# Attention with a routed feed-forward: the softmax is normalised on GpSimd before the transposes instead of behind the product with the values

## What is computed

```python
q = (layernorm(x) @ Wq.T + bq)   # 16 heads of 32
k = (ctx @ Wk.T + bk);  v = (ctx @ Wv.T + bv)
scores = q k^T / sqrt(32) + mask
attn = softmax(scores, axis=-1)
x = x + tanh(g_xattn) * ((attn @ v) @ Wo.T + bo)
# then, on layernorm(x): gate_weights = softmax(x @ gate_w + gate_b), the two
# best of 8 experts, each a network of three layers with gelu between them
x = x + tanh(g_ffn) * sum(topk_vals * expert_out[topk_idx])
```

## Time and profile before

| | us |
|---|---|
| median of 3 runs (lowest, highest) | 1741.77 (1741.31, 1743.95) |
| the profiled execution | 1747.38 |
| its span | 1745.6 |
| TensorE busy | 1714.5 (98%) |
| VectorE busy | 1209.6 (69%) |
| ScalarE busy | 932.3 (53%) |
| GpSimd busy | 181.0 (10%) |
| granted TensorE clock, mean | 0.995 |

### The profile page before, as it was taken

The page is one execution under the profiler, slowest core; times in us unless marked ns, Lnnn a source line. Parts: engine busy times, 40 slices in busy tenths (PEclk is TensorE's granted clock), DMA queues, the critical chain, the costliest instruction groups (busy, mean ns, idle before and its releaser), DMA issues.

```text
span 1745.6 us, 40414 instructions
## 1 busy us (share of the span) xinstructions
PE 1714.5 (98%) x15462; PEld 1515.4 (87%) x15462; DVE 1209.6 (69%) x2807; ACT 932.3 (53%) x1652; POOL 181.0 (10%) x271
## 2 busy tenths in 40 slices
PE   9998999999999999999999999999999999999998
PEld 8887988898888888988897777777899999999997
DVE  5576777777777777777775555666677777777773
ACT  5654565556555655565554344545555555555551
POOL 1011110111011101110100010000000010011100
PEclk9999999999999999999999999999999999999999
DMA  7983222322132213221215299998666666766662
GB/s 247 383 313 101 72 81 60 98 73 85 56 99 74 80 59 99 72 85 55 77 34 181 74 365 395 351 349 296 218 212 204 207 210 216 223 223 221 212 199 49
DMA packets 128181, 292.72 MB, mean 168 GB/s; under 512 B 19610, under 2 KB 42842, under 8 KB 128040
## 3 DMA queue, kind: packets, MB, share of 16 engines
q1 hardware_dynamic: 104616, 225.46, 38.3%
q0 software_dynamic: 23424, 65.30, 12.6%
HBM read 244.04 MB, written 46.66 MB: 167 GB/s over the span
## 4 chain that ended last, share of the span: by engine, by line
PE 82%; DVE 8%; DMA 5%; ACT 3%; issue 2%; SPq 0%; POOLq 0%; DVEq 0%; POOL 0%; ACTq 0%
PE bank_rows L2289 21%; PE bank_rows L739 12%; PE bank_rows L725 12%; PE bank_rows L2304 7%; PE bank_rows L792 5%; PE bank_rows L2343 3%; PE bank_rows L780 3%; PE bank_rows L803 3%; PE bank_rows L2329 3%; PE bank_rows L819 3%; DVE probs L1458 3%; PE bank_rows L762 2%; PE bank_rows L2370 2%; DMA stage<-in_L_ffn_w 2%; PE bank_rows L882 2%
## 5 line engine op out<-in xcount | busy, mean ns | idle before, releaser
L1136 ACT ACTIVATE probs<-probs,neg_max 100x726 f32<-100x726 f32 x256 | 228.9, 896 | 176.2 <-DVE neg_max L1458 176.2
L1458 DVE CUSTOM_DVE_ANT_0 probs<-bank_rows,mask_sb 100x726 f32<-100x726 f32 x256 | 223.0, 909 | 23.2 <-PE bank_rows L780 20.4
L2533 DVE TENSOR_TENSOR w_low<-stage,w_high 128x1024 fp32r<-128x1024 f32 x176 | 213.4, 1223 | 36.2 <-ACT w_high L2437 35.5
L2437 ACT ACTIVATE w_high<-stage 128x1024 fp32r<-128x1024 f32 x176 | 183.6, 1057 | 33.7 <-DMA stage<-in_L_ffn_w 33.6
L2460 ACT ACTIVATE gelu<-bank_rows,biases 128x256 f32<-128x256 f32 x176 | 82.4, 475 | 216.7 <-PE bank_rows L2289 173.8
L2289 PE MATMUL bank_rows<-h_high,w_high 128*128 128x256 f32 x704 | 196.5, 279 | 0.0
L2289 PE MATMUL bank_rows<-h_low,w_high 128*128 128x256 f32 x704 | 196.5, 279 | 0.0
L2289 PE MATMUL bank_rows<-h_high,w_low 128*128 128x256 f32 x704 | 196.5, 279 | 0.0
L1142 ACT ACTIVATE p_t<-bank_rows 122x1200 f32<-122x1200 f32 x128 | 146.5, 1169 | 91.3 <-PE bank_rows L792 91.3
L725 PE MATMUL bank_rows<-ctx_high,wk_high 128*128 128x360 f32 (+1 forms) x512 | 176.9, 346 | 10.7 <-DVE v_even L1439 8.4
L725 PE MATMUL bank_rows<-ctx_low,wk_high 128*128 128x360 f32 (+1 forms) x512 | 168.9, 330 | 0.0
(11 more groups left out here) (245 smaller groups left out, 3862.3 us busy)
## 6 DMA issues: line engine op xcount, KB each, us to landing
stage<-in_L_ffn_w SPq DMA_DIRECT2D x240, 512.0 KB, 4.4
plain_w<-in_L_ffn_w SPq DMA_DIRECT2D x15, 2048.0 KB, 12.5
expert_in_rows<-filling POOLq DMA_DIRECT2D x8, 3341.0 KB, 23.0
router_rows<-in_gate_rows POOLq DMA_DIRECT2D x112, 200.0 KB, 3.6
ctx_raw<-in_ctx SPq DMA_DIRECT2D x16, 720.0 KB, 4.7
ctx_raw<-in_ctx SPq DMA_DIRECT2D x15, 724.0 KB, 4.3
xs_sb<-expert_in_rows SPq DMA_DIRECT2D x11, 514.0 KB, 5.5
b_sb<-in_L_ffn_b SPq DMA_DIRECT2D x19, 256.0 KB
```

The costliest lines, as they stand in the source:

```text
L1136: nc.scalar.activation(p, p, ACT.Exp, bias=neg_max[:, h:h + 1], scale=-1.0, accum_out=exp_sum[:, h:h + 1]).then_inc(probs_ready, 1)
L1458: nc.vector.tensor_tensor_reduce(out=pieces(probs[:, q, :]), in0=slots_of(q)[0:S, :, 0:PIECE], in1=pieces(mask_sb[:]), scale=-1.0, scalar= ...
L2437: nc.scalar.activation(hi, src, ACT.Copy).then_inc(chunk_hi[which], 1)
L2533: nc.vector.tensor_tensor(lo, src, hi.bitcast(F32), ALU.subtract).then_inc(chunk_lo[which], 1)
```

## The change

The exponentials are multiplied by the inverse of their sum before they are transposed, by GpSimd, in place. VectorE inverts the sums of a pair (`invert`, 100x2) as soon as its order comes to it, GpSimd's `divide` multiplies one head at a time, and `transpose_probs` waits for `probs_divided` instead of `probs_ready`. The transpose of the inverse, its broadcast and its copy are gone, and `scale_o` has become `copy_o`, a plain copy. In `body`, one unit stands between the two transpose runs of a group, on TensorE and in ScalarE's order. On ScalarE the key copy of the last unit is behind all four exponentials in group 1, and `route_exps` is ahead of a key copy in group 2. On GpSimd the loops over batches are written out, with the fills spread over batches 0 and 1 and the wait for them in batch 2.

```diff
@@ on_gpsimd @@
-        for e in range(E):
-            pool.wait_ge(scored, FILL_AFTER[e])
...
-        pool.wait_ge(regions_filled, 16 * E)
...
+        def divide(b, g):
+
+            for h in range(HQ * g, HQ * (g + 1)):
+                if h % 2 == 0:
+                    pool.wait_ge(sum_inverted, H // 2 * b + h // 2 + 1)
+                p = probs[:, h % HQ, :]
+                nc.gpsimd.tensor_scalar(p, p, recip[:, h:h + 1], None, ALU.mult).then_inc(probs_divided, 1)
+
+        def body(b, t):
+
+            if b == 2:
+                pool.wait_ge(regions_filled, 16 * E)
+            if b > 1:
+                scatter(t - 1)
+            if b == 1:
+                fill(E - 4)
+            divide(b, 0)
+            if b == 1:
+                fill(E - 3)
+            divide(b, 1)
+            pass_router(t, (0,))
+            pass_router(t, (1, 2))
+            if b == 1:
+                fill(E - 2)
+            divide(b, 2)
+            pass_router(t, (3,))
+            if b == 1:
+                fill(E - 1)
+            divide(b, 3)
+            pass_router(t, range(4, E if t < IN_ROWS - 1 else E - ROUTER_SLOTS))
+
+        for g in range(DT):
+            pool.wait_ge(scored, HQ * g + 1)
+            fill(g)
+            divide(0, g)
@@ on_tensor @@
         def transpose_probs(b, pair):
-            pe.wait_ge(probs_ready, H * b + 2 * pair + 2)
+            pe.wait_ge(probs_divided, H * b + 2 * pair + 2)
@@ attend @@
-            pe.wait_ge(recip_ready, DT * b + g + 1)
-            nc.tensor.transpose(bank[:, P:P + S], recip_sum[:].rearrange("s h d -> s (h d)"),
-                                ident[0:S, 0:S]).then_inc(ready, 1)
+            last.then_inc(ready, 1)
@@ body of on_tensor, group 2 @@
             transpose_probs(b, 4)
-            transpose_probs(b, 5)
             if b + 2 < B:
                 transpose_xn(b, b + 2)
             keys(b, n, *((1, 0) if odd else (0, 1)))
+            transpose_probs(b, 5)
             keys(b, n, 0 if odd else 1, 1)
@@ body of on_scalar, group 2 @@
             copy_probs(b, 4)
-            copy_probs(b, 5)
             if b + 2 < B:
                 copy_transposed(b, "XT", xt[:, :, slot(b + 2), :])
+            route_exps(t)
             keys_high(b, n, *((1, 0) if odd else (0, 1)))
-            route_exps(t)
+            copy_probs(b, 5)
             keys_high(b, n, 0 if odd else 1, 1)
@@ on_vector @@
-        def recips(b, g):
-            dve.wait_ge(probs_ready, H * b + HQ * (g + 1))
-            at = slice(HQ * g, HQ * (g + 1))
-            nc.vector.reciprocal(recip[:], exp_sum[:, at]).then_inc(recip_made, 1)
-            dve.wait_ge(recip_made, DT * b + g + 1)
-            nc.vector.tensor_copy(recip_sum[:], recip[:].rearrange("s (h a) -> s h a", a=1).broadcast_to([S, HQ, HD])
-                                  ).then_inc(recip_ready, 1)
-
-        def scale_o(body, b, g):
+        def invert(b, pair):
+
+            dve.wait_ge(probs_ready, H * b + 2 * pair + 2)
+            at = slice(2 * pair, 2 * pair + 2)
+            nc.vector.reciprocal(recip[:, at], exp_sum[:, at]).then_inc(sum_inverted, 1)
+
+        def copy_o(body, b, g):
             bank, done = take(body, f"A{g}")
-            dve.wait_ge(r_copied, DT * b + g + 1)
-            nc.vector.tensor_tensor(o_t[:, g, :], bank[:, 0:S], r_sb[:], ALU.mult).then_inc(done, 1)
+            nc.vector.tensor_copy(o_t[:, g, :], bank[:, 0:S]).then_inc(done, 1)
@@ body of on_vector, groups 2 and 3 @@
             scored_around(b, 2, b, b, 1)
+            invert(b, 4)
             keys_low(b, n, 2, 0)
+            invert(b, 5)
             dots(t, (3, 4))
-            recips(b, 2)
             values_out(b, 1 - odd, 1)
...
             scored_around(b, 3, b, b, 2)
+            invert(b, 6)
             keys_low(b, n, 3, 0)
+            invert(b, 7)
             choose(t)
-            recips(b, 3)
             values_out(b, 1 - odd, 2)
```

More of the change, by code:

```diff
@@ L936, in body @@
             transpose_probs(b, 0)
+            values(b, 4)
             transpose_probs(b, 1)
-            values(b, 4)
             values(b, 5)
@@ L949, in body @@
             transpose_probs(b, 2)
+            if odd:
+                values(b, 0)
+            else:
+                keys(b, n, 0, 0)
             transpose_probs(b, 3)
             if odd:
-                values(b, 0)
                 keys(b, n, 0, 0)
             else:
-                keys(b, n, 0, 0)
                 keys(b, n, 1, 0)
@@ L1119, in copy_transposed @@
                                  ACT.Copy).then_inc(done, 1)
-        def recip_copy(body, g):
-            bank, _ = take(body, f"A{g}")
-            nc.scalar.activation(r_sb[:], bank[:, P:P + S], ACT.Copy).then_inc(r_copied, 1)
         def queries_high(body, name):
@@ L1220, in body @@
             exps(b, 0)
-            recip_copy(b, 3)
             exps(b, 1)
@@ L1699, in first_body @@
             norm_in(1)
-            recips(b, 0)
             values_out(b, 0, 4)
@@ L1709, in first_body @@
             ctx_low(n, 3)
-            recips(b, 1)
             keys_low(b, n, 0, 0)
@@ L1802, in last_body @@
             scored_around(b, 0, b, t, 3)
+            invert(b, 0)
             keys_low(b, b, 3, 1)
-            recips(b, 0)
+            invert(b, 1)
             values_out(b, odd, 3)
```

101 lines of the change are left out of this document (49 added, 52 removed).

## The result

| | before | changed |
|---|---|---|
| median of the runs (lowest, highest), us | 1741.54 (1740.82, 1743.95) | **2085.57** (2082.75, 2091.07) |
| ratio, 95% interval | 1 | 1.1976 (1.1949 to 1.2004) |
| profiled execution and its span, us | 1747.4 and 1745.6 | 2086.4 and 2084.6 |
| busy TensorE, VectorE, ScalarE, GpSimd, us | 1714.5, 1209.6, 932.3, 181.0 | 1828.9, 1256.0, 923.7, 750.2 |
| granted TensorE clock, mean | 0.995 | 0.938 |

A forecast was written before the change was run, and what follows sets the result against it. TensorE was taken as the bound, busy 299.06 of 300 us in the attention part. Middle batches +38.5, first and last batch +21, clock +5, fills -8 gave +56.5 on 1741.8: 1798 us, range 1762 to 1832.

The forecast's parts named there:

- Part 1: Every group: the inverse is no longer transposed, giving TensorE 0 to 0.24 us a group, 0.12 taken.
- Part 2: GpSimd's 256 multiplies of 100x726: 0.85 us each, bounds 0.73 and 1.46; groups 0 to 2 lose nothing up to 0.86.
- Rival B: A slow multiply on GpSimd: at 1.1 us +29, so 1827 us; at 1.46, near 1870; chance 0.15.
- Part 3: Group 3: the choice of experts starts later and TensorE's pair count waits for it; the group ends 1.15 us later.
- Part 4: Group 2: late values and a router row reloaded behind four multiplies delay group 3's scores by 1.8 us a period.
- rival A: VectorE and GpSimd hold each other up at router dots and the choice of experts: +24.5 us, so 1823; chance 0.25.
- Part 5: First and last batch: transpose runs wait for divided pairs in eight places at 2.6 us, +21 us; clock falls, +5.
- Clock: First and last batch: TensorE's clock falls twice more after waits, +5 us, with 0 and eight falls as bounds.
- Part 6: Batch 1: a later wait for the fills, spread over two batches, shortens TensorE's gap: -8 us, bounds -4 and -9.
- the count: TensorE's count of the pairs in group 3, waiting for the choice of experts: 1.15 us later a period.
- C: Faster: freed VectorE lets inverse, multiply and router row arrive before TensorE asks; 1739 us, chance 0.06.

## Why the prediction was wrong

The sign was right, but not for the reason given: most of the cost comes from a multiply 2.6 times as long as the sum's. By its own parts:

- **Part 1** (0 to 0.24 us a group, 0.12 taken): at the low end. Without multiplies and in the old order the kernel is at 0.9981, no better than with the fills alone, 0.9988. VectorE's wait in the midst of its scores is gone, and it was off the path.
- **Part 2 is the step that failed**: "I take 0.85 us ... bounds 0.73 and 1.46". The multiply takes 2.1 us, 2.24 in the mean, outside the bounds. The memset and the copy were the nearest rows, but not an upper bound for an instruction that reads, computes and writes: its price an element is 2.51 ns, where the memset's 518 ns are 1.0 ns an element at most. An upper bound made of twice a write had no row behind it that reads a long stream on GpSimd. Rival B added 29 us to the sum for a multiply of 1.1 us, which makes 86 in all; 124 were measured at 1.17 us. That is 1866 us, near the 1870 that B gave to a multiply of 1.46.
- **The rule in part 2**, no first run of groups 0 to 2 late up to 0.86 us, held at 0.84 us: no such wait in the middle batches.
- **Part 3** (16 us): 15 us by the kernel with group 3 put back. **Part 4** (25 us): 24 us by the one with group 2 put back. But these are costs of the order, not of the multiply: they are there with no multiply at all, which the text did not see. That part 4 fits so well is in part luck, since its 25 us were worked out with a multiply of 0.85 us. With one of 0.84 us group 2 waits for 33 us, and the 8 us more are about the 9 that VectorE's dots add to the second pair (rival A).
- **Part 5** (21 us in eight places): 19.4 us in eight waits at 0.84 us. At 2.24 us batch 0 alone has 5.82, 4.08, 4.87 and 5.96 us. Clock: +5 with bounds 0 and eight falls. At the predicted length it was more: TensorE is busy for 1733.0 us at a mean clock of 0.986, and for 1716.8 at 0.995 with no multiplies, 16 us less for the same work. In the changed kernel about 8 us of every period are lower clock, which my sum had nowhere, since it had no waits of 2 to 3 us in the middle batches.
- **Part 6** (-8): -2. The text had the wait on GpSimd's side end the gap; the queue behind the fill held the row as well.

At the length that it assumed, the sum was off by 18 us. Against its terms group 2 has 8 us more, the fills 6 and the clock 11, the count 4 less and the first and last batch 2 less, which makes 19. At the real length it was off by 288, and nearly all of that is the multiply: waits for GpSimd (198.7 us where the sum had 21), the scores behind the router's row (38.9 where it had 25), and the clock that these waits bring down (14 x 8 = 112 us where it had 5). Against them stands the count, which waits 0.9 us instead of 16.

**Rival A** (VectorE and GpSimd hold each other up) was right as a mechanism, and smaller than forecast. The run with 8 columns shows it best. An undisturbed pair of multiplies takes 0.59 us; the pair that starts beside VectorE's two subtractions of context halves takes 1.99 and ends 0.45 us after them, while the subtractions take what they always take. GpSimd first, then VectorE:

```profile
535.09 0.59 POOL L563 TENSOR_SCALAR probs<-probs,recip 100x8 f32<-100x8 f32 x2 [5.69 <-DVE recip L1487]
536.28 1.99 POOL L563 TENSOR_SCALAR probs<-probs,recip 100x8 f32<-100x8 f32 x2 [0.60 <-DVE recip L1487]
```

```profile
536.10 1.72 DVE L1439 TENSOR_TENSOR ctx_low<-ctx_raw,ctx_high 128x724 fp32r<-128x724 f32 x2
```

By the Trainium skill (SBUF — State Buffer, section "SBUF: two separate sides") a VectorE instruction with two SBUF inputs and a GpSimd one that reads exclude each other, and whichever starts first is done first; the trace agrees. At full length it also goes the other way: dots of at most 694 ns without multiplies take up to 1449 ns. In size it is nearly the same at every length: mean less median is 157, 142, 157 and 130 ns a multiply at 8, 162, 290 and 726 columns, 33 to 40 us over all 256, but 61 ns with the constant; at full length the dots are 12 us longer in all. What it costs in time is read from the chain at 162 columns: in group 2 of the middle batches the second pair is held up by 0.65 us or more, 9 us in all, where rival A gave 24.5. That is a reading of the chain and not a measurement: no kernel here took it away and kept the rest. Rivals B and C: B was the right one, with an end (1.46 us) that was too short; nothing came of C.

What the prediction said would show it: L806 is gone, and the scores of group 3 wait for ScalarE's copy. But the multiplies are not near 0.85 us, TensorE waits at first runs in every group, and the count hardly waits, since everything else is later. By its own words, "a multiply above 1.1 us, or TensorE waiting for a first pair in groups 0 to 2", it was wrong.

## What to carry to other kernels

An operation that an engine has never done in the trace has no upper bound from its cheaper neighbours: give it a wide range (2.24 us were 2.6 times the 0.85 taken here), find the length at which its cover ends (here 0.86 us), and put the sum beyond that point among the forecasts, since past it every further microsecond costs several times what it did before. Price a reordering by itself, with nothing to wait for: the waits that it makes (35 us here) are paid whether or not the thing that it makes room for needs the room. And before work is moved off the busiest engine, look whether the small instruction that is saved there was on the path at all: 64 transposes of the inverse were worth less than these runs can tell from zero, about 2 us.

## What the runs showed of the hardware

- GpSimd's in-place multiply of 100 rows of fp32 by one factor a row costs 0.29 us and 2.51 ns an element, straight from 8 to 726 columns; a constant in place of the row's factor saves 75 ns at 726. ScalarE does the same 100x726 in 0.893 us.
- A short GpSimd instruction can be held by a long VectorE one that reads two tiles of SBUF: 0.59 us for a pair became 1.99. Beside two dot products a pair at 162 columns took 2.04 us in place of 1.39.
- Waits of 1 to 3 us, six in 80 us, bring TensorE's granted clock to 0.93 in the mean of 300 us, with stretches of 4 us at 0.51. With eight waits of 2 to 3.5 us in about 93 us, in the old order with full multiplies, it was 0.80. With three waits of 0.7 to 1.8 us a period at 162 columns it stayed at 1.00 from 300 to 900 us.
